# The keys' rotation as two products around the swap, in a buffer of its own, with all stages of a decoder layer at new places

## The reference, cut to what matters

```python
x = layernorm(x + mamba(x))          # selective scan: 256 inner channels, 16 states
x = layernorm(x + retention(x, ctx)) # one head, causal decay mask, rotated q and k
x = layernorm(x + moe(x))            # 16 experts of 64, top 2, and a shared expert

def _xpos(x, offset, inverse_scale):     # the rotation of q and of k
    rot = stack((-x[..., 1::2], x[..., ::2])).reshape(x.shape)  # neighbours swapped
    return x * cos + rot * sin
k = _xpos(ctx @ Wk.T, 0, True)
retention = (q @ k.T) * mask;  out = retention @ v
```

## Time and profile before

| | |
|---|---|
| median of 3 runs | 1138.42 us (1136.34 to 1139.41) |
| the profiled execution | 1136.04 us, span of its profile 1134.1 us |
| busy in the span | DVE 92%, PE 91%, ACT 87%, POOL 87% |

### The profile page before, as it was taken

One profiled execution on the slowest core, in us unless ns is written; L12 is line 12 of the kernel. 1 busy time (PEld: TensorE's weight loads), 2 busy tenths in 40 slices (PEclk: granted clock), 3 DMA queues, 4 the chain that ended last, 5 costly groups with the idle time before them and its releaser, 6 DMA issues. The chain is left out here.

```text
span 1134.1 us, 18240 instructions
## 1 busy us (share of the span) xinstructions
PE 1030.5 (91%) x5831; PEld 732.6 (65%) x5831; DVE 1048.2 (92%) x1458; ACT 991.2 (87%) x2159; POOL 989.4 (87%) x608
## 2 busy tenths in 40 slices
PE   4786888999999999999999999999999999989897
PEld 2464656676766767676676767666676767666665
DVE  2999999999999999999999999999999999999521
ACT  6779798999999999999999999999999999898442
POOL 0577798999989898998989899898989999898854
PEclk9678899999999999999999999999999999999999
DMA  6544454555546465555646465554645555552221
GB/s 161 210 155 160 166 171 176 181 186 177 193 169 197 160 191 184 187 179 178 207 152 203 164 197 187 177 191 168 213 171 191 191 179 186 178 186 106 84 94 52
DMA packets 84111, 194.49 MB, mean 171 GB/s; under 512 B 17288, under 2 KB 47936, under 8 KB 67632
## 3 DMA queue, kind: packets, MB, share of 16 engines
q1 hardware_dynamic: 84016, 193.33, 50.7%
HBM read 179.14 MB, written 5.77 MB: 163 GB/s over the span
## 5 line engine op out<-in xcount | busy, mean ns | idle before, releaser
L937 POOL TENSOR_TENSOR read<-state,bc_all 128x1024 f32<-128x1024 f32 x256 | 605.2, 2366 | 92.4 <-DVE state L811 85.5
L811 DVE TENSOR_TENSOR_SCAN state<-decay,drive_bank 128x512 f32<-128x512 f32 (+1 forms) x464 | 594.2, 1315 | 1.9 <-issue 0.2
L761 ACT ACTIVATE decay<-delta,a_neg 128x252 f32<-128x252 f32 x1024 | 422.5, 494 | 0.9
L803 DVE TENSOR_TENSOR drive_bank<-dx_bank,bc_all 128x512 f32<-128x512 f32 (+1 forms) x496 | 329.9, 702 | 2.6 <-DMA bc_all<-bc_dram 2.5
L373 PEld LDWEIGHTS y_bank<-ident,read 128*128 128x128 f32 x2048 | 239.8, 145 | 88.2 <-POOL read L937 47.4
L373 PE MATMUL y_bank<-ident,read 128*128 128x128 f32 x2048 | 275.8, 279 | 22.1 <-POOL read L937 21.9
L982 POOL TENSOR_TENSOR hid<-gu,comb_all 128x512 f32<-128x512 f32 (+1 forms) x136 | 165.0, 1214 | 17.7 <-DVE gu L897 12.4
L364 PEld LDWEIGHTS down_bank<-down_w,hid 128*128 128x128 f32 x1024 | 127.0, 192 | 30.4 <-issue 27.5
L731 ACT ACTIVATE silu<-bank 128x512 f32<-128x512 f32 (+1 forms) x153 | 87.8, 576 | 57.8 <-PE bank L364 55.1
L364 PE MATMUL down_bank<-down_w,hid 128*128 128x128 f32 x1024 | 135.8, 277 | 1.5 <-POOL hid L982 1.5
L364 PE MATMUL bank<-x2T,up_w 128*128 128x512 f32 (+1 forms) x272 | 132.1, 570 | 0.5 <-ACT silu L731 0.5
(11 more groups left out here) (127 smaller groups left out, 1356.0 us busy)
## 6 DMA issues: line engine op xcount, KB each, us to landing
bc_all<-bc_dram SPq DMA_DIRECT2D x128, 1024.0 KB, 4.9
comb_all<-comb_dram SPq DMA_DIRECT2D x240, 128.0 KB, 4.1
x_in<-in_x_dram SPq DMA_DIRECT2D x15, 256.0 KB, 5.4
ctx_in<-in_ctx_dram SPq DMA_DIRECT2D x15, 256.0 KB, 5.5
k_pair<-k_pair SPq DMA_DIRECT2D x30, 128.0 KB, 2.5
q_pair<-q_pair SPq DMA_DIRECT2D x30, 128.0 KB, 2.1
out_dram<-y_out SPq DMA_DIRECT2D x15, 256.0 KB, 6.0
comb_all<-comb_dram SPq DMA_DIRECT2D x32, 64.0 KB, 2.6
```

The lines of the kernel that those rows point to most:

```text
L761: done = e.activation(seqs(decay_t[j % DECAYS][:, i, h, :])[:, :, 1:T], seqs(delta[c % 2][:, h, sub * SUB:(sub + 1) * SUB])[:, :, 1:T], AC ...
L803: e.tensor_tensor(drive_bank[:, a:b, :, :], dx_bank[:, :, :].unsqueeze(1).to_broadcast(shape), bc_all[group % BC_BUFS][:, 0, PAIR * i + a: ...
L811: e.tensor_tensor_scan(states(state_t[j % STATE_BUFS], a, b), states(decay_t[j % DECAYS], a, b), states(drive_bank, a, b), 0.0, ALU.mult, ...
L937: e.tensor_tensor(read_t[j % READS][:, :, :, :], state_t[j % STATE_BUFS][:, :, :, :], bc_all[group % BC_BUFS][:, 1, PAIR * i:PAIR * (i + 1 ...
```

## The change

It has two parts. The first changes the keys. `k_rot` (128x1024) becomes two instructions of 128x512: `k_cos` multiplies `k_pair[:, 0]` by the cosines into a new buffer `k_sum` and needs only `k_copy`, and `k_rot` multiplies the swapped half by the sines and needs the swap. `k` adds into `k_sum`, `score_mm` reads `k_sum`, and `k_copy` of a chunk waits for the sum of the chunk before (`k`) in place of its `score_mm`; that wait is now on `k_cos`. The second gives nearly all entries of the table new ticks, most by one to five, some more, and new places to the decays.

```diff
 AT = {
-    "k_mm": [(67, 67)],
+    "k_mm": [(64, 61)],
...
-    "k_rot": [(72, 71)],
-    "k": [(91, 78)],
+    "k_cos": [(71, 63)],
+    "k_rot": [(69, 65)],
+    "k": [(94, 78)],
...
-    "k_swap": [(69, 51)],
+    "k_swap": [(59, 51)],
...
-LAST_EXP_AT = [-9, -9, -7, -6, -2, 4, 16, 20]
+LAST_EXP_AT = [-11, -5, -2, 1, 5, 14, 15, 16]
...
+        k_sum = sb("k_sum", [P, CHUNK])
...
-                        done = mm(bank.t[:, cols], k_pair[:, 0, cols], q_pair[:, 0, cols])
+                        done = mm(bank.t[:, cols], k_sum[:, cols], q_pair[:, 0, cols])
...
-                    w.wait_ge(S["score_mm"], at(c - 1))
+                    w.wait_ge(S["k"], at(c - 1))
                     copy(k_pair[:, 0, 0:width(c)], bank_of["k", c][:, 0:width(c)]).then_inc(S["k_copy"], 1)
...
+                for c in due(tick, "k_cos"):
+                    w.wait_ge(S["k_copy"], at(c))
+                    w.wait_ge(S["score_mm"], at(c - 1))
+                    e.tensor_tensor(k_sum[:, 0:width(c)].rearrange("p (b t) -> p b t", t=T),
+                                    k_pair[:, 0, 0:width(c)].rearrange("p (b t) -> p b t", t=T),
+                                    xpos[:, 2, :].unsqueeze(1).to_broadcast([P, width(c) // T, T]), ALU.mult).then_inc(S["k_cos"], 1)
                 for c in due(tick, "k_rot"):
                     w.wait_ge(S["k_swap"], at(c, 1, 2) * 16)
-                    pair = k_pair[:, :, 0:width(c)].rearrange("p i (b t) -> p i b t", t=T)
-                    e.tensor_tensor(pair, pair, xpos[:, 2:4, :].unsqueeze(2).to_broadcast([P, 2, width(c) // T, T]),
+                    turned = k_pair[:, 1, 0:width(c)].rearrange("p (b t) -> p b t", t=T)
+                    e.tensor_tensor(turned, turned, xpos[:, 3, :].unsqueeze(1).to_broadcast([P, width(c) // T, T]),
                                     ALU.mult).then_inc(S["k_rot"], 1)
                 for c in due(tick, "k"):
+                    w.wait_ge(S["k_cos"], at(c))
                     w.wait_ge(S["k_rot"], at(c))
-                    e.tensor_tensor(k_pair[:, 0, 0:width(c)], k_pair[:, 0, 0:width(c)], k_pair[:, 1, 0:width(c)], ALU.add).then_inc(S["k"], 1)
+                    e.tensor_tensor(k_sum[:, 0:width(c)], k_sum[:, 0:width(c)], k_pair[:, 1, 0:width(c)], ALU.add).then_inc(S["k"], 1)
```

More of the change, by code:

```diff
@@ L64 @@
[L64 to L73, removed]
-    "x2T": [(120, 101)],
[L75 to L82, removed]
@@ L101 @@
[L101 to L105, removed]
+    "xT_mm": [(-48, -44)],
+    "tap_mm": [(-37, -36)],
+    "xb_mm": [(-41, -43)],
+    "proj_mm": [(-32, -30)],
+    "dt_mm": [(-20, -20)],
+    "ctxT_mm": [(59, 23)],
+    "k_mm": [(64, 61)],
+    "v_mm": [(62, 66)],
+    "out_mm": [(69, 67)],
+    "q_mm": [(77, 68)],
+    "r1_var_mm": [(85, 75)],
+    "score_mm": [(97, 87)],
@@ new lines @@
+    "retout_mm": [(106, 91)],
+    "x2T_mm": [(123, 94)],
+    "router_mm": [(127, 100)],
+    "combT_mm": [(135, 122)],
+    "xT": [(-46, -46)],
+    "conv_bias": [(-43, -41)],
+    "proj": [(-29, -30)],
+    "ctxT": [(56, 16)],
+    "v": [(64, 68)],
+    "k_copy": [(65, 65)],
+    "x1T": [(72, 70)],
+    "q_copy": [(78, 71)],
+    "r1_var": [(84, 74)],
+    "ret_copy": [(99, 80)],
+    "square2": [(108, 88)],
+    "normed2": [(114, 98)],
+    "x2T": [(120, 101)],
+    "combT": [(136, 121)],
+    "square3": [(193, 229)],
@@ new lines @@
+    "normed3": [(204, 334)],
+    "xc0": [(-37, -38)],
+    "xc1": [(-32, -33)],
+    "delta": [(-17, -18)],
+    "top_tanh": [(131, 106)],
+    "tap1": [(-39, -37)],
+    "tap2": [(-38, -36)],
+    "tap3": [(-35, -35)],
+    "rstd2": [(108, 92)],
+    "rstd3": [(196, 318)],
+    "k_cos": [(71, 63)],
+    "k_rot": [(69, 65)],
+    "k": [(94, 78)],
+    "q_rot": [(83, 71)],
+    "q": [(90, 77)],
+    "ret": [(101, 79)],
+    "bc_store": [(-30, -35)],
+    "k_swap": [(59, 51)],
+    "q_swap": [(74, 68)],
@@ L106 @@
+    "comb_store": [(134, 118)],
+    "x_load": [(-59, -65)],
+    "ctx_load": [(-56, -70)],
+    "store": [(219, 309)],
+    "z_mm": [(11, 32), (39, -26)],
+    "gate_z": [(10, 39), (38, 39)],
+    "y_gated": [(39, 52), (69, -21)],
+    "yT_mm": [(59, 58), (69, -32)],
+    "yT": [(58, 62), (66, -28)],
+    "dx": [(-15, -14), (18, -21)],
+    "dx_bank": [(-6, -5), (31, -62)],
     "gate_mm": [
-        (135, 134), (141, 137), (142, 157), (151, 161), (157, 189), (163, 203), (176, 226), (178, 243), (179, 286)],
+        (136, 137), (140, 142), (142, 148), (151, 148), (157, 186), (163, 186), (176, 196), (178, 215), (178, 277)],
@@ L114 @@
+    "gu": [(143, 126), (149, 132), (156, 156), (160, 158), (169, 223), (181, 223), (185, 252), (187, 301)],
+    "hid": [(143, 132), (148, 136), (162, 158), (166, 174), (181, 175), (182, 249), (183, 283), (187, 306)],
     "down_mm": [
[L115 to L118, removed]
@@ L119 @@
-    "up_copy": [(136, 119)],
-    "shared": [(142, 132)],
+        (144, 156), (157, 168), (163, 228), (175, 246), (177, 278), (182, 289), (185, 305), (188, 335), (192, 335)],
+    "comb_load": [(137, 136), (137, 151), (139, 178), (141, 182), (146, 188), (149, 197), (161, 233), (172, 265)],
+    "pick": [(134, 106)],
+    "weigh": [(134, 112)],
+    "up_copy": [(136, 120)],
+    "shared": [(139, 132)],
 }
@@ L123 @@
 WHOLE_SCANS = (3, 6, 14)
[L124 to L125 removed]
+EXP_AT = [-11, -9, -5, -4, 1, 4, 6, 15, 18, 24, 32, 33, 36, 41, 45, 52]
+LAST_EXP_AT = [-11, -5, -2, 1, 5, 14, 15, 16]
 class Passed:
@@ L258, in decoder_layer @@
             "decay", "drive", "state", "read", "y", "y_gated", "yT_mm", "yT", "out_mm",
-            "x1T", "r1_sq", "r1_var_mm", "r1_var", "ctxT_mm", "ctxT", "k_mm", "k_copy", "k_swap", "k_rot", "k", "v_mm", "v", "q_mm", "q_copy", "q_swap", "q_rot", "q",
+            "x1T", "r1_sq", "r1_var_mm", "r1_var", "ctxT_mm", "ctxT", "k_mm", "k_copy", "k_swap", "k_cos", "k_rot", "k", "v_mm", "v", "q_mm", "q_copy", "q_swap", "q_rot", "q",
             "score_mm", "ret_copy", "ret", "retout_mm", "x2T_mm", "x2T", "router_mm", "router", "top_tanh",
```

37 lines of the change are left out of this document (2 added, 35 removed).

## The result

The changed kernel takes 1153.85 us (median of 4 runs, 1152.30 to 1155.15) where the kernel before takes 1138.44 (1136.34 to 1139.41). The ratio is 1.0145, with an interval of 1.013 to 1.016. That is 15.4 us slower, where 1.6 us faster was forecast, with 1142.5 as the upper end of the range.

A forecast was written before the change was run, and what follows sets the result against it. The prediction took DVE as the bound in the steady part, then POOL for a few steps, then PE. Its terms, -1.7 + 0.7 - 0.6 = -1.6 us, gave 1136.8 us against the median of 1138.42, range 1133.0 to 1142.5.

The forecast's parts named there:

- the keys' part: Keys on POOL, each chunk: `k_rot` goes into a 2.67 us hole behind `rstd3`; DVE gains nothing in the steady part.
- rival (1): Steady part: a late swap makes `k_rot` hold up a `read`; +16.5 us, 1153 us, a third of it 1142; chance 0.06.
- `silu` ahead of `y_out`, -1.7: First routed expert, ACT: `gu`'s wait of 0.14 us goes in 12 of 16 chunks, -1.7 us; bounds 0 and -3.7.
- the matmul is as late: Bound of 0 for `silu`'s new place: `gu` gains nothing because its matmul comes as late.
- rival (3): Faster: DVE's listed waits and PE's idle time in the tail both go; -4.8 us, 1133.6 us; chance 0.18.
- The head, +0.7: Head: two table loads delay the second `xc` by 2.9 us; 2.49 us of DVE waiting hides most, leaving +0.7 us.
- The prediction's other figure, +3.4: Head, by the skill's page: a drain of about 1380 ns follows each table load, about +3.4 in place of +0.7.
- my outer bound of +2.9: Head: upper bound, where the 2.9 us shift reaches the scan in full.
- The tail, -0.6: Tail: POOL hands over the last `read` 0.7 us earlier, PE carries it on, 0.1 lost; -0.6 us, bounds -1.8 and +2.6.
- The keys in two products, +0.2 a chunk, hidden: POOL, each chunk: two products for one cost +0.20 us, 3.2 us over 16 chunks, covered by POOL's idle time.
- (4): Rival: slower in the tail or the head by their outer bounds; +3.8 us, 1142.2 us; chance 0.06.
- (2): Rival: `gu` too early on DVE waits 0.3 us in each chunk; +4.5 us, above 1141.3 us; chance 0.08.

The follow-up runs named there:

- e1: Changed kernel with the sines' product moved behind the `read` and the cosines' product (tick 69 to 71): 1142.08 us, ratio 1.0045.
- e10: Kernel before plus one POOL product of 128x512 on an unused scratch tile behind `rstd3` in each full chunk: 1148.13 us.
- e2: Changed kernel with the cosines' product in POOL's hole behind `rstd3` and the sines' product behind the `read`: 1154.23 us.
- e5: Kernel before with only the keys' two products, both at the old place, and the third buffer: 1137.65 us, ratio 0.9999.
- e6: Kernel before plus two POOL memsets on an unused scratch tile behind `rstd3` in each full chunk: 1137.56 us.
- e8: Changed kernel with the sines' product behind the `read` and the first `xc` behind the exponential again: 1138.64 us, ratio 1.0016.
- e7: Kernel before with only the head's exponential placed between the two `xc`: 1139.97 us.
- e4: Changed kernel with the first `xc` behind the exponential again: 1150.02 us, ratio 1.0113.
- e12: e8 with the fifth tile's gate and up products ahead of the `y` product that waits for a `read`, in chunk 14 alone: 1137.51 us, ratio 1.0003.

## Why the prediction was wrong

**The step that failed** is in the keys' part: "In the steady part this lies beside DVE's work". I asked of the new place only what POOL waits for and who waits for POOL. On that the step was right in each point: the product lies between `rstd3` and a `read` that still waits (2.58 us), the swap is in time, and rival (1) didn't happen. What I didn't ask is what DVE runs in those 2.67 us. The hole exists because DVE is busy there with something that makes no scan, its routing, and that is the one block of small instructions with two SBUF inputs. The section of the Trainium skill named above speaks against just this; the prediction leaves it out, and has no rival for it. In place of nothing a chunk the runs show about 1.0: 15 times (1129 - 225) ns = 13.6 us, and 11.4 us of the time come back by one place (e1). e10 shows it in the kernel before with a foreign product; e2 and e5 show that swap, halves and buffer don't matter. That reading is what blocks and not POOL's activity rests on e6 and e10, one profiled run each, and one instruction doesn't fit: `rstd` also reads SBUF, is under way for 1.01 us, and leaves `above` beside it at 0.23.

**`silu` ahead of `y_out`, -1.7.** The sum was about right, by luck; its working wasn't. In e8, where nothing covers it, DVE's stretch is 1.0 us shorter. But the chunks don't lose a wait of 0.14 each: they take 65.18 us for 65.13. In e8 `silu` is over at 653.92 and `gu` still starts 0.10 late, at 654.24, behind the matmul that ends at 654.14: the prediction's own lower bound, "the matmul is as late". The gain lies in two of the first chunks (63.13 to 62.33 and 66.34 to 65.16), where the two listed waits of `gu` for PE are gone. I had argued in rival (3) that these would stay. The gain is more than scatter: `gu` has no listed wait in the changed kernel, e1 and e8, and 2.1 to 2.3 us of it in e5, e6 and e7, which keep the old places; their stretches take 1031.7 to 1033.5 us, those of e1 and e8 1030.3 and 1030.4. Which move took the waits away wasn't tried.

**The head, +0.7.** ACT's part was right: two loads of 1.28 us with the next instruction 1.29 behind each, no drain. The prediction's other figure, +3.4, which took a drain behind each load, meets the measured +3.4 by luck. What failed is "the 2.49 us of waiting hid most of it": this reserve was read from a trace in which PE was fast. In the traces with the exponential first and PE's product at 1.93 us, the first decay starts at 21.95 to 22.37 us and not at 19.42, and of the wait for B and C 0 to 0.6 us is left, where the fast ones have 1.7 to 2.5. The first `drive` is at 29.75 to 30.59 in all nine. PE's slowness alone is thus hidden, and by the same rows most of a shift of 2.9 us on ACT alone would be; together they aren't. The second `xc` came 3.8 us later ("the first `xc` waits for PE until 13.17 as before" fell too, it was 14.04, behind a convolution product of 3.54 us for 2.89), the chain over PE behind it took 2.1 more, so decays and centring moved by some 6 us and not 2.9, and the first `drive` came at 33.19, with no wait for a transfer. Alone it measured +3.1 at the first `drive` and +3.7 at the end (e7, one run), beyond my outer bound of +2.9. What the exponential costs with PE fast no run shows, nor whether its longer wait (3.83 us for 0.87) is why PE was slow in five of five. The 0.6 us by which e4 and e8 stay behind the trace of before lie within the scatter of the nine.

**The tail, -0.6.** POOL's part came as reckoned (-0.8 for -0.7), and goes when the sines' product goes behind the `read` (e1). That PE "carries it on" didn't: work that stood ahead of the `y` product stands behind it, PE has nothing to do while it waits for the `read`, and runs the next 4 us at 0.5 to 0.6. Its `y` and gate products there take 1.97 and 1.51 us for 1.09 and 1.02, 1.4 in all of the 1.7. e2, with the same order and the same pause, was slow for longer and lost 1.9 more, so it is the clock that costs, and how long it stays down differs from run to run. e12 takes 1.7 us out of the tail by filling the pause, nearly all of the 2.0 that e8 loses there; as it moves 2.0 us of PE's work ahead of the `read`, it can't tell the pause from the clock by itself.

**The keys in two products, +0.2 a chunk, hidden.** Right: e5 is at 0.9999.

**Rivals.** (1) named 1153 us, nearly the measured time, but for a late swap, which isn't there: the number is a coincidence. (4) had the head at +2.9 and was nearest in kind, but gave 1142.2 us. (2), a `gu` that comes too early, isn't there: DVE's listed waits went down to 0.6 us.

## What to carry to other kernels

An idle stretch of one engine is made by what another does in it: before filling it, list the other engine's instructions there with the memory of each operand, and for a GpSimd instruction that reads SBUF keep clear of VectorE's with two SBUF inputs. Such a loss shows in no wait and no idle time, only in the mean of one shape, so compare the groups with shapes kept apart. And a reserve read in one trace (here 2.49 us of waiting in the head) is that run's: read it in several before hiding a delay behind it, above all where the chain crosses TensorE.

## What the runs showed of the hardware

- A VectorE instruction of 0.23 us (SBUF, SBUF to SBUF) that starts 0.06 us behind a GpSimd product of 1.26 us takes 1.28 us, and the profile counts it as busy. One that started 0.02 us ahead of such a product took 0.22.
- Two GpSimd memsets of 128x512 (0.53 us each) in the same place lengthened none. Neither did the 1.01 us of `rstd`, a power of 128x4 with two SBUF inputs, beside `above`, which also has two (0.23 us). Its duration is long and its data small; whether that is the reason wasn't tried.
- GpSimd products beside VectorE's `drive`, scan and `gu`, each with an operand in PSUM, left these as long as in the trace of before: a scan 2.32 us for two, `gu` 0.67, in the changed kernel too. In the trace of before the scan at 646.75 took 1.21 us with POOL idle, and the mean of all 416 of that size is 1.20, with POOL busy for 87% of the span.
- In the tail the granted clock of TensorE was 0.62 and 0.52 behind a pause of 2.31 us that followed one of 0.45, and 0.50 behind one of 3.74; behind pauses of 1.27, 1.98 and 2.15 us (e12, before, e5) in the same stretch it was 1.00.
- With the same places and a pause of 2.29 us it was 0.62, 0.50, 0.50 and 0.68 in the four windows of 2 us from 1072 on (e2), where the changed kernel had 0.62, 0.52, 1.00 and 1.00: how long it stays down isn't the program's alone.
- In the head the same four products of 128x256 took 1.06 us in four traces and 1.93 in ten, and the granted clock of the windows was 1.00 in some of either.
